# Turning small tiles by transposing DMAs instead of TensorE, in a two-layer transformer kernel on one core

## What is computed

```
inter = xf @ c1_w.T @ c2_w.T                 # 512 -> 16 -> 1792
blk = inter.reshape(B * T, n_blocks, SPARSITY)   # 56 blocks of 32
idx = jnp.argmax(blk, axis=-1) + jnp.arange(0, INTER, SPARSITY)
w1_g = w1[idx]
w2_g = w2t[idx]
h = jax.nn.relu(jnp.einsum('bkm,bm->bk', w1_g, xf))
out = jnp.einsum('bk,bkm->bm', h, w2_g)
```

## Time and profile before

| | us |
|---|---|
| median of 3 runs | 749.77 (748.33 to 750.22) |
| the profiled execution | 748.2 |
| its span in the trace | 746.1 |
| TensorE busy | 726.7 (97%) |
| VectorE busy | 477.8 (64%) |
| ScalarE busy | 212.9 (29%) |
| GpSimd busy | 155.8 (21%) |

### The profile page before, as it was taken

How to read it: one execution, slowest core, us unless ns; L and a number is a source line. 1 busy time by engine, 2 the same in 40 slices (tenths; PEclk the granted TensorE clock), 3 DMA queues, 4 the chain that set the end, 5 groups by cost and what they waited for, 6 DMA issues and landing times.

```text
span 746.1 us, 12177 instructions
## 1 busy us (share of the span) xinstructions
PE 726.7 (97%) x3431; PEld 331.4 (44%) x3431; DVE 477.8 (64%) x916; ACT 212.9 (29%) x340; POOL 155.8 (21%) x132
## 2 busy tenths in 40 slices
PE   6999999999999999999999999999999999999994
PEld 2444444444444444444444444444444444444442
DVE  4887687697867779688867879653655361124115
ACT  1645367435721211112112111222212221122210
POOL 0433452211111111111111111222122212222210
PEclk9999999999999999999999999999999999999998
DMA  9448309410000000100003350104110005001001
GB/s 323 184 130 251 56 5 339 109 56 1 1 15 15 16 16 0 29 15 15 1 15 76 59 103 5 30 2 99 44 41 1 0 15 141 0 1 57 0 1 56
DMA packets 35364, 43.37 MB, mean 58 GB/s; under 512 B 19974, under 2 KB 27782, under 8 KB 34438
## 3 DMA queue, kind: packets, MB, share of 16 engines
q1 hardware_dynamic: 33222, 38.78, 17.5%
q0 software_dynamic: 2112, 4.19, 3.3%
HBM read 34.33 MB, written 4.44 MB: 52 GB/s over the span
## 4 chain that ended last, share of the span: by engine, by line
PE 84%; DVE 8%; issue 3%; DMA 1%; ACT 1%; SPq 1%; ACTq 0%; DVEq 0%; POOL 0%
PE acc L454 28%; PE pb L440 20%; PE pa L440 20%; PE acc L519 10%; DVE sc L1365 2%; DVE big L1033 1%; PE acc L737 1%; DMA big<-in_x_t 1%; DVE big L1357 1%; DVE work L1229 1%; PE pick_a L502 1%; ACT big L881 1%; PE pick_b L573 1%; PE pick_a L573 1%; DVE small L1246 1%
## 5 line engine op out<-in xcount | busy, mean ns | idle before, releaser
L454 PE MATMUL acc<-big,work 128*128 128x512 f16 (+1 forms) x1104 | 248.4, 379 | 0.6
L942 POOL TENSOR_TENSOR work<-work 128x512 f32 (+1 forms) x96 | 112.3, 1172 | 506.2 <-ACT work L861 278.2
L440 PE MATMUL pa<-xs,big 128*128 128x512 f16 (+1 forms) x816 | 188.9, 379 | 0.7 <-DVE work L1229 0.7
L440 PE MATMUL pb<-xs,big 128*128 128x512 f16 (+1 forms) x816 | 187.2, 379 | 0.1
L454 PEld LDWEIGHTS acc<-big,work 128*128 (+1 forms) x1104 | 107.7, 98 | 130.0 <-issue 4.3
L440 PEld LDWEIGHTS pb<-xs,big 128*128 128x128 f16 (+1 forms) x816 | 78.6, 98 | 91.8 <-issue 0.2
L440 PEld LDWEIGHTS pa<-xs,big 128*128 128x128 f16 (+1 forms) x816 | 78.0, 98 | 90.7 <-issue 1.2
L919 ACT ACTIVATE work<-work 128x512 f32 x56 | 35.2, 628 | 219.7 <-DVE work L1470 216.7
L519 PE MATMUL acc<-big 128*128 128x512 f16 x336 | 73.7, 379 | 0.6 <-POOL big L949 0.6
L1470 DVE SCALAR_TENSOR_TENSOR work<-big,const_sb,pa 128x512 f32<-128x512 f16 (+1 forms) x28 | 20.8, 745 | 83.2 <-PE pa L440 82.9
L861 ACT ACTIVATE work<-work 128x512 f32 (+1 forms) x40 | 25.2, 630 | 158.1 <-DVE work L1229 158.1
(11 more groups left out here) (140 smaller groups left out, 513.8 us busy)
## 6 DMA issues: line engine op xcount, KB each, us to landing
big<-in_w_all SPq DMA_DIRECT2D x2, 3840.0 KB, 16.9
big<-spread_rows SPq DMA_DIRECT2D x16, 448.0 KB, 6.9
big<-in_x_t SPq DMA_DIRECT2D x16, 256.0 KB, 4.0
rows<-in_x POOLq DMA_DIRECT2D x4, 1024.0 KB, 10.0
big<-in_w_all SPq DMA_DIRECT2D x2, 1536.0 KB, 10.2
out<-rows SPq DMA_DIRECT2D x3, 1024.0 KB, 5.0
big<-in_w_all SPq DMA_DIRECT2D x1, 2048.0 KB, 16.1
big<-in_w_all SPq DMA_DIRECT2D x2, 1024.0 KB, 5.3
```

The source lines that it names most:

```text
L440: mm = nc.tensor.matmul(dst[:, :], weights(wp)(kc * P, P), x_part16(g, xp, kc), start=(kc == 0 and wp == xp), stop=(kc == KC - 1 and wp == 1))
L454: mm = nc.tensor.matmul(acc[t][:, :], act_part(pair, j, ap, t * P, P), weights(wp)(0, H), start=(first and ap == wp), stop=(last and ap == 1))
L942: nc.gpsimd.tensor_tensor(act_part(pair, j, 1), act32[j], act_part(pair, j, 0), ALU.subtract).then_inc(act_lo, 1)
```

## The change

Both transposes on TensorE and both copies on VectorE go. SP issues a transposing DMA for the picks (`turn_winner`), waits for it, stores the result, and then issues a transposing DMA for z (`turn_z`), which TensorE waits for before score 0. The two identity matrices are no longer made. The picks of tile i are now sent ahead of z of tile i+1 in the same `send`; `load_spread(0)` comes one `send` later and `load_spread(1)` behind the `send` of tile 11. `pe.Fori` becomes Python's `range` throughout, so all of TensorE's program is written out.

```diff
@@ block.sync
-            def store_turned(i):
-
-                sp.wait_ge(turned_copied, i + 1)
-                sp.dma_start(spread_rows[:, i * P:(i + 1) * P], turned).then_inc(spread_out, 16)
-
-            def turned_stored(i):
-
-                sp.wait_ge(spread_out, 16 * (i + 1))
-                sp.sem_inc(turned_free, 1)
+            def turn_winner(i):
+
+                sp.wait_ge(winner_ready, i + 1)
+                if i:
+                    sp.wait_ge(spread_out, 16 * i)
+                sp.dma_start(turned, winner[:, (i % 2) * P:(i % 2 + 1) * P], transpose=True).then_inc(winner_turned, 16)
+                sp.wait_ge(winner_turned, 16 * (i + 1))
+                sp.dma_start(spread_rows[:, i * P:(i + 1) * P], turned[0:BLOCKS, :]).then_inc(spread_out, 16)
+
+            def turn_z(i):
+
+                sp.wait_ge(z_cut, i + 1)
+                sp.dma_start(z_stack, z_split, transpose=True).then_inc(z_turned, 16)
...
             def send(i, nxt=True):
 
-                store_turned(i)
+                if i:
+                    turn_winner(i - 1)
+                turn_z(i)
                 if nxt:
                     turn_x1(i + 1)
-                turned_stored(i)
-                if nxt:
                     x1_arrived(i + 1)
...
             x1_arrived(0)
-            for i in range(LAST * TPG - 3):
+            for i in range(LAST * TPG - 2):
                 send(i)
             sp.wait_ge(gate_ready, LAST * C1 + 7)
             load_spread(0)
-            for i in range(LAST * TPG - 3, LAST * TPG - 1):
-                send(i)
+            send(LAST * TPG - 2)
+            send(LAST * TPG - 1, False)
             sp.wait_ge(hid_ready, 1)
             load_spread(1)
-            send(LAST * TPG - 1)
+            turn_x1(LAST * TPG)
+            x1_arrived(LAST * TPG)
             send(LAST * TPG)
...
@@ block.tensor
-            def turn_winner(i, dst):
-
-                pe.wait_ge(winner_ready, i + 1)
-                nc.tensor.transpose(dst[:, :].bitcast(F16)[:, H:H + P],
-                                    winner[:, bass.ds(((i + 1) % 2) * P, P)], ident16[:, :]).then_inc(winner_turned, 1)
-
-            def turn_z(tile, dst):
-
-                pe.wait_ge(z_cut, tile + 1)
-                nc.tensor.transpose(dst[:, :].bitcast(BF16)[:, 0:P], z_split, ident_bf[:, :])
-                turn_winner(tile, dst)
-
             def scores(tile, k, dst):
 
                 if k == 0:
-                    pe.wait_ge(z_stacked, tile + 1)
-                    pe.wait_ge(turned_copied, tile + 1)
+                    pe.wait_ge(z_turned, 16 * (tile + 1))
...
-                    if tile is not None:
-                        if j == 0:
-                            turn_z(tile, pick_a)
-                        else:
-                            scores(tile, 2, pick_a)
+                    if tile is not None and j == 1:
+                        scores(tile, 2, pick_a)
...
-                with pe.Fori(2, U1) as u:
+                for u in range(2, U1):
...
-            with pe.Fori(1, GROUPS - 1) as g:
+            for g in range(1, GROUPS - 1):
...
@@ block.vector
-            def copy_turned(i, src):
-
-                dve.wait_ge(winner_turned, i + 1)
-                dve.wait_ge(turned_free, i + 1)
-                v.tensor_copy(turned, src[:, :].bitcast(F16)[0:BLOCKS, H:H + P]).then_inc(turned_copied, 1)
-
-            def stack_z(tile, src):
-
-                dve.wait_ge(winner_turned, tile + 1)
-                v.tensor_copy(z_stack, src[:, :].bitcast(BF16)[:, 0:P]).then_inc(z_stacked, 1)
-                copy_turned(tile, src)
-
```

More of the change, by code:

```diff
@@ L77 @@
 PEAK_X1, PEAK_W1, PEAK_W2 = 2, GROUPS + 1, GROUPS + 2
-SPREAD_TILES = GROUPS * TPG + 1
+SPREAD_TILES = GROUPS * TPG
 class Steps:
@@ L124, in program @@
         const_sb = sb("const_sb", [P, CONST_COLS], F32)
-        ident16 = sb("ident16", [P, P], F16)
-        ident_bf = sb("ident_bf", [P, P], BF16)
         rev_wide = sb("rev_wide", [P, PICK_COLS], F16)
@@ L220, in program @@
         winner = big16[:, a16 + 2496:a16 + 2496 + 2 * P]
-        turned = big16[0:BLOCKS, a16 + 2752:a16 + 2752 + P]
+        turned = big16[:, a16 + 2752:a16 + 2752 + P]
         assert a16 + 2752 + P <= 2 * W1_AT
@@ L248, in program @@
         spread_in = [sem(f"spread_in{g}") for g in range(GROUPS)]
-        turned_free = sem("turned_free")
-        winner_ready, winner_turned, turned_copied = sem("winner_ready"), sem("winner_turned"), sem("turned_copied")
+        winner_ready, winner_turned, z_turned = sem("winner_ready"), sem("winner_turned"), sem("z_turned")
         u_ready, delta_pre_ready, taylor_ready = sem("u_ready"), sem("delta_pre_ready"), sem("taylor_ready")
@@ L276, in program @@
         x1_ready, x1_lo, score_used = sem("x1_ready"), sem("x1_lo"), sem("score_used")
-        z_cut, z_stacked = sem("z_cut"), sem("z_stacked")
+        z_cut = sem("z_cut")
         c1_scaled, c1_lo = sem("c1_scaled"), sem("c1_lo")
@@ L387, in load_spread @@
                 at = 2 * (W1_AT + 7 * W1_SLOT) - (g % 2) * 8 * W1_SLOT
+                sp.wait_ge(spread_out, 16 * TPG * (g + 1))
                 dst = big16[:, at:at + C2 * GT].rearrange("p (c t) -> p c t", c=C2)
-                src = spread_rows[:, (g * TPG + 1) * P:((g + 1) * TPG + 1) * P].rearrange("(c b) t -> b c t", b=BPC)
+                src = spread_rows[:, g * TPG * P:(g + 1) * TPG * P].rearrange("(c b) t -> b c t", b=BPC)
                 for b in range(BPC):
@@ L420, in _ @@
             send(LAST * TPG + 3, False)
-            send(LAST * TPG + 4, False)
+            turn_winner(LAST * TPG + 3)
             sp.wait_ge(masked, 2 * C2)
@@ L699, in s @@
                 return go
-            def zt(tile):
-                return lambda: turn_z(tile, pick_a)
             def z2(tile, g, t):
@@ L707, in _ @@
             tile = (GROUPS - 1) * TPG - 1
-            unit2(0, 0, none, zt(tile), s(tile, 0, 1), "phase 1", start=True, between=z2(tile, GROUPS - 2, TPG - 1))
+            unit2(0, 0, none, none, s(tile, 0, 1), "phase 1", start=True, between=z2(tile, GROUPS - 2, TPG - 1))
             s(tile, 2)()
-            with pe.Fori(0, 2) as g:
+            for g in range(2):
                 for i in range(2):
@@ L716, in _ @@
                     unit2(g, 2 * i + 2, s(tile - 1, 3) if i else none, none, none, "middle")
-                    unit2(g, 2 * i + 3, none, zt(tile), s(tile, 0, 1), "middle", between=z2(tile, GROUPS - 1, g * 2 + i))
+                    unit2(g, 2 * i + 3, none, none, s(tile, 0, 1), "middle", between=z2(tile, GROUPS - 1, g * 2 + i))
                     s(tile, 2)()
@@ L723, in _ @@
                 unit2(g, 1, s(GROUPS * TPG - 1, 3) if g == 2 else none, none, none, "first")
-                if g == 2:
-                    turn_winner(GROUPS * TPG, pick_b)
-                with pe.Fori(2, U2 if g == 2 else U2 - 1) as u:
+                for u in range(2, U2 if g == 2 else U2 - 1):
                     unit2(g, u, none, none, none, "middle")
@@ L1413, in _ @@
             dve.wait_ge(w2_lo, 2 * C2 + 4)
-            v.tensor_scalar(winner.rearrange("p (a c) -> p a c", a=2), ident32.unsqueeze(1).broadcast_to([P, 2, P]),
-                            0.0, None, ALU.mult).then_inc(winner_ready, 1)
+            step(v.tensor_scalar(winner.rearrange("p (a c) -> p a c", a=2), ident32.unsqueeze(1).broadcast_to([P, 2, P]),
+                                 0.0, None, ALU.mult))
             def unit1(g, u, tile, nxt=None):
@@ L1420, in unit1 @@
                 swiglu(g, u, 0)
-                stack_z(tile, pick_a)
                 if nxt is not None:
@@ L1512, in _ @@
                 first_unit(g, GROUPS * TPG - 1 if g == 2 else None, 2, rows_out)
-                if g == 2:
-                    copy_turned(GROUPS * TPG, pick_b)
                 with dve.Fori(2, U2) as u:
```

3 lines of the change are left out of this document (removed).

## The result

| | before | after |
|---|---|---|
| median of 5 runs each, us | 748.37 (748.33 to 750.22) | 755.95 (755.48 to 756.72) |
| the profiled execution | 748.2 | 756.5 |
| its span | 746.1 | 754.4 |

What follows compares the result with a forecast made beforehand. TensorE, busy 97% of the span, was taken as the bound. Gains 1.7 + 1.6 + 0.4 less 0.3 and 0.9 made 2.5 us: 747.3 us against the median of 749.8, range 745.3 to 753.5.

Steps and rivals of the forecast that it cites:

- Transposes, 1.7: On TensorE: removing the transposes of z and picks, 0.11 us a pair, would gain 1.7 us.
- the copies on VectorE: On VectorE: removing the copies, 0.2 us each, would bring nothing, since it then waits for ScalarE anyway.
- Gaps, 1.6: On TensorE behind score 2: written-out code would close a gap of 0.26 us in six units, gaining 1.6 us.
- Rival 3: Gaps behind score 2 stay, caused by semaphore waits and not register instructions: gain 1.5, 748.3 us; chance 0.07.
- First product with C1, 0.4: On TensorE after the x1 wait: written out, its small matmuls without register instructions would gain 0.4 us.
- Instruction fetch, 0.3: About 10 more blocks over the instruction queue may delay small turns on DMA engines: 0.3 us lost, bounds 0 and 1.
- Rival 5: Instruction fetch stalls TensorE, 10 more blocks at 0.5 us each: a loss of 2.5 us, 752.3; chance 0.05.
- The slack and how waits add up: At score 0: slack 3.92 us against need 0.63 + 2T; every second tile in a row waits, loss 0.9 us.
- T = 1.75: On SP: a 128x128 transposing DMA was taken to land in 1.75 us, between outer bounds of 1.3 and 2.4.
- Rival 1: A turn takes as long as x1's, 2.4 us: waits of 7.8 us, result 754.2, slower; chance 0.13.
- Tile 10, "up to 0.8": At tile 10, with load_spread(0) ahead of its turns: up to 0.8 us of wait, in a unit that waits for VectorE anyway.
- The end-of-phase wait: At the end of phase 1 TensorE waits for VectorE's SwiGLU anyway, 0.74 us plus the pair gone, absorbing tile 10's wait.

Runs made afterwards that it cites:

- experiment 3: The changed kernel with z turned ahead of the winner and the picks' rows again 4352 bytes apart; 745.22 us, the second time 743.37.
- experiment 4: The kernel before with TensorE's four loops written out and nothing else; 745.37 us, ratio 0.9953.
- experiment 8: The changed kernel with TensorE's four loops put back; 757.5 us, ratio 1.0116.
- experiment 1: The changed kernel with only the row distance of the picks put back, 4352 bytes and no longer 4096; 749.55 us, ratio 1.0017.
- experiment 5: The kernel of experiment 3 with 18 more DMAs on SP, each waited for, in a quiet stretch of phase 2; a 128x128 turn landed after 2.2 us.
- experiment 2: The changed kernel with z turned ahead of the winner in SP's queue, nothing else; 747.8 us, ratio 0.9990.
- experiment 6: The kernel before with rows of picks 8192 bytes apart instead of 4352; 759.09 us in one run.

## Why the prediction was wrong, by its own steps

- **Transposes, 1.7: right.** Tiles 1 to 9 gained 2.4 us without waits (experiment 3), the written-out loops alone 1.4 of it (experiment 4), so 9 pairs cost 1.0, or 0.11 each. With the loops' share these gains make up the sum, so nothing is left for the copies on VectorE.
- **Gaps, 1.6: right.** They closed in all six units, and in the kernel before by writing out alone. Rival 3 falls. The register instructions are not the whole of it: put back in experiment 8, they cost nothing where TensorE had waited at score 0.
- **First product with C1, 0.4: too small.** It gave 1.0.
- **Instruction fetch, 0.3: nothing showed.** The 10 more blocks came as reckoned, and idle time stands only at places with a semaphore. Rival 5 falls.
- **The slack and how waits add up: right.** With T = 2.29 the need is 0.63 + 4.58 = 5.2 against a slack of 3.92: the pattern would be 1.3, 0.3, 1.0, and measured were 1.2, 0.1, 1.0 in tiles 1 to 3, 1.1, 0.05, 1.0 in 5 to 7 and 0.8 in tile 9, in sum 5.3.
- **T = 1.75: wrong, the first failed step.** I had an x1 turn of the same kind with 2.4 and took 0.65 off it for its fewer packets, though no row of a second size showed that the rest stays the same. It does not: the piece behind the packets grew from 0.4 to 0.9. This makes 5.3 us of waits out of 0.9. Rival 1 had the mechanism, with almost these waits, at a chance of 0.13. The Trainium skill's rule that I cited against the change (DMA: Bandwidth & Descriptors, section "Anatomy of one DMA — SWDGE (gpsimd) path", about 2.0 of fixed cost; 2.1 for this turn as an estimate) was nearer to the 2.3 than my split of the row. It is written for GpSimd's queue, and its constant is larger than the small store's 1.3 to 1.4. With this step alone wrong, the time would be about that of experiment 1, 749.55, inside the range.
- **Tile 10, "up to 0.8": wrong, the second failed step, and the larger one.** Two things were missed. The prediction weighed the load's new place only by the x1 turns' 4.7 us, and not by the landing of the load itself (9.1 us before), behind which a turn comes down. And the row distance was not weighed at all. The wait became 5.66; with the row distance alone put back it is 1.24.
- **The clock: not in the sum at all.** The 5.66 us of wait were followed by 2.5 us lost at the lower level. The end-of-phase wait, about 1.0, was absorbed as forecast.

The working again, with measured terms: gains 4.5 (1.5 in tile 0's unit, 2.4 in tiles 1 to 9, 0.6 in the rest); losses 5.4 in tiles 1 to 9, 7.0 at the seam, 0.3 ahead of tile 0. The net is 8.2, and the span grew by 8.3.

Open: why a turn's landing hardly depends on its size, and what makes a row distance slow. Only sizes from 16x128 to 128x512 were measured.

## What to carry to other kernels

Before replacing two small operations of the bounding engine by DMAs, take a transposing DMA at the nearest measured duration whole, not scaled by its bytes, and multiply by those that stand in a row on one queue; put the urgent one first. A small DMA behind a bulk load on one queue landed with the load here (430.8 behind 430.5 in the changed kernel, 427.5 behind 427.2 in experiment 1), so price the load's landing, and treat every constant in the address of a DRAM buffer as part of the change. A long wait of TensorE can cost the matmuls after it as well: 1.5 to 2.8 us after the waits of 3.6 us and more at the seam.

## What the runs showed of the hardware

- A transposing DMA from SBUF to SBUF (experiment 5): 1.10 us of issue and 2.2 to landing for 128x128 as for 16x128, 2.4 for 128x512; a plain copy of 128x128 0.48 and 1.7.
- A load of 4 x 448 KB with rows gathered from DRAM: its last DMA lands 8.9 to 10.4 us after issue with rows 4352 bytes apart, 13.2 to 15.7 at 4096, 17.9 to 19.2 at 8192.
- After waits of 3.6, 5.7, 6.0 and 6.2 us at tile 10 (experiment 2, the changed kernel, experiments 8 and 6) TensorE's next matmuls ran at 1.2 GHz, for 1.5, 2.5, 2.8 and 2.8 us of loss; after a wait of 1.2 us (experiment 1) they did not. The length of one wait doesn't settle it: in the initial loads the changed kernel waited 3.0 us until 16.5 with the clock at 1.00 behind it, experiment 3's kernel 2.2 until 16.7 with 0.51 from 17 to 20 us.
- With a register instruction ahead of each, four small matmuls took 0.67 us right behind a wait of TensorE and the next four 0.52; written out they take 0.10.
